# Two-layer graph network on one core: 16-bit count sums widened by ScalarE, the first power alone, a merge step inside a wait, the first aggregate's halves taken together

## The reference

```
# layer block 0: graph convolution, batch norm, gelu, twice the input added, layer norm
deg  = segment_sum(ones, col)            # reference adds one loop per node again
norm = rsqrt(deg)[row] * rsqrt(deg)[col]
h    = segment_sum(norm * (x @ W.T)[row], col) + b
h    = gelu(batch_norm(h, gamma, beta)) + x
x    = layernorm(x + h)
# layer block 1: two gated relational layers over 2 edge types
w[r] = sum_b att[r, b] * basis[b]        # 30 bases of 512 x 512 each, per layer
msg  = sigmoid(x_j @ gate_w[r]) * x_j @ w[r]      # r is the edge's type
h    = relu(segment_sum(msg, row) + x @ root1 + bias1)
out  = the same with basis2, att2, gate_w2, root2, bias2 on h
return layernorm(x + out)
```

## Time and profile before

| | |
|---|---|
| three runs | 316.65, 318.35, 320.71 us |
| median | 318.35 us |
| the profiled execution | 318.3 us |
| its span in the profile | 316.2 us |
| TensorE busy | 278.1 us, 88% of the span |
| VectorE, ScalarE, GpSimd busy | 161.4, 87.4, 40.3 us |
| mean granted clock of TensorE | 0.957 of full |
| moved by DMA | 73.63 MB |

### The profile page before, as it was taken

How to read it: one execution, slowest core, us unless ns; L and a number is a source line. 1 busy time by engine, 2 the same in 40 slices (tenths; PEclk the granted TensorE clock), 3 DMA queues, 4 the chain that set the end, 5 groups by cost and what they waited for, 6 DMA issues and landing times.

```text
span 316.2 us, 4593 instructions
## 1 busy us (share of the span) xinstructions
PE 278.1 (88%) x1687; PEld 184.8 (58%) x1687; DVE 161.4 (51%) x362; ACT 87.4 (28%) x137; POOL 40.3 (13%) x76
## 2 busy tenths in 40 slices
PE   1698958999699987659999999999997999999991
PEld 1583423343487554236766646677775777787770
DVE  3888888884575842983320141342425125334443
ACT  5250220201145848445152114111312242100000
POOL 2001000000294104510000000000004600010000
PEclk9999996999859997899999999999999999999997
DMA  6997992999938999986994977977101400001112
GB/s 174 241 417 295 338 403 82 410 379 401 367 86 274 343 421 419 423 313 262 335 399 158 421 287 288 425 282 262 77 0 43 126 0 0 0 2 32 32 32 65
DMA packets 12802, 73.63 MB, mean 233 GB/s; under 512 B 2000, under 2 KB 2243, under 8 KB 4588
## 3 DMA queue, kind: packets, MB, share of 16 engines
q1 hardware_dynamic: 11330, 70.82, 59.1%
q0 software_dynamic: 1104, 2.36, 2.7%
q10 hardware_dynamic: 346, 0.17, 0.2%
HBM read 72.05 MB, written 1.28 MB: 232 GB/s over the span
## 4 chain that ended last, share of the span: by engine, by line
PE 66%; DVE 12%; DMA 9%; issue 6%; DVEq 3%; SPq 1%; ACT 1%; POOL 1%; POOLq 0%; ACTq 0%
PE psW L495 15%; PE psM L476 9%; PE psM L478 8%; PE psM L477 8%; PE psM L720 7%; PE psM L740 6%; DMA basis_ring<-in_L_gnn_basis_dram 5%; DVE B L1037 3%; DMA w_raw<-in_L_gnn_W_dram 3%; PE psM L617 3%; PE psE L576 2%; PE psM L543 2%; DVEq L1027 2%; DVE oh_key L1044 1%; PE psM L599 1%
## 5 line engine op out<-in xcount | busy, mean ns | idle before, releaser
L495 PE MATMUL psW<-basis_ring,S 128*32 128x512 f32 x512 | 64.8, 624 | 5.4 <-DMA basis_ring<-in_L_gnn_basis_dram 3.3
L1216 DVE SCALAR_TENSOR_TENSOR zg<-psM,gate,zg 125x512 fp32r<-125x512 f32 x20 | 15.0, 750 | 56.9 <-ACT zg L893 56.9
L495 PEld LDWEIGHTS psW<-basis_ring,S 128*32 128x32 f32 x512 | 13.6, 112 | 38.8 <-issue 29.0
L476 PE MATMUL psM<-w,hlT 128*125 128x512 f32 x80 | 32.4, 406 | 0.1
L478 PE MATMUL psM<-w,hlT 128*125 128x512 f32 x80 | 31.7, 396 | 0.0
L477 PE MATMUL psM<-w,hlT 128*125 128x512 f32 x80 | 31.6, 395 | 0.0
L576 PEld LDWEIGHTS psE<-oh_key,oh_src 128*125 128x125 f16 x162 | 14.2, 146 | 22.4 <-issue 15.2
L893 ACT ACTIVATE zg<-psM,gate 125x512 fp32r<-125x512 f32 x20 | 13.8, 689 | 46.3 <-PE psM L478 45.9
L720 PEld LDWEIGHTS psM<-BB,zg 125*128 125x128 f32 x160 | 23.1, 188 | 3.4 <-issue 2.5
L720 PE MATMUL psM<-BB,zg 125*128 125x320 f32 (+1 forms) x160 | 24.1, 309 | 0.0
L740 PE MATMUL psM<-zg,BB 125*125 125x512 f32 x100 | 24.0, 394 | 0.0
(11 more groups left out here) (152 smaller groups left out, 383.2 us busy)
## 6 DMA issues: line engine op xcount, KB each, us to landing
basis_ring<-in_L_gnn_basis_dram SPq DMA_DIRECT2D x64, 1024.0 KB, 6.9
root_raw<-in_L_gnn_root_dram POOLq DMA_DIRECT2D x32, 64.0 KB, 2.1
xs<-in_x_dram SPq DMA_DIRECT2D x1, 1120.0 KB
out_dram<-xs SPq DMA_DIRECT2D x5, 224.0 KB
w_raw<-in_L_gnn_W_dram SPq DMA_DIRECT2D x4, 256.0 KB, 9.2
bias_b<-in_L_gnn_bias_dram POOLq DMA_DIRECT2D x1, 250.0 KB, 3.8
xs<-in_x_dram SPq DMA_DIRECT2D x1, 130.0 KB
out_dram<-xs SPq DMA_DIRECT2D x5, 26.0 KB
```

Source lines behind the costliest of these rows:

```text
L476: nc.tensor.matmul(o, l_hi, r_hi, start=start, stop=False)
L495: m = nc.tensor.matmul(psW[32 * j:32 * j + 32, cc % 2, :], S[:, cc % 2, cc // CH, q].rearrange("p k r -> p (k r)"), ring[:, n % RING, j, : ...
L1216: link(v.scalar_tensor_tensor(out=zg[:, 1, c, r, :], in0=bank(("Z", L, c, r))[0:PC, :], scalar=gate[:, L, c, r:r + 1], in1=zg[:, 0, c, r, ...
```

## The change

- **Counts.** The sums of chunks 1, 2 and 3 are written by VectorE as 16-bit numbers into memory of the one-hots (`at_sums`), and ScalarE widens them into `AT`. Chunks 0 and 4 are added directly as before. VectorE's order is 1, 2, 0, 3, 4; TensorE's degree matmuls go in the order 1, 0, 2, 3, 4, and each group waits for its own chunk (`wait_at`).
- **Powers.** GpSimd takes the power of the first column alone, then of the other four. ScalarE and VectorE start `z` of chunk 0 on the first. The five `diag` products become one of 625 elements.
- **Merge.** The second merge is cut in two. Its first step stands between the count sums and the wait for the degrees, the rest between the degree copy and `z`.
- **First aggregate.** For f = 0 both halves are taken together, chunk by chunk; the `dinv` matmuls come behind both. The bank uses of `dinv` move likewise.
- **Weight parts.** A pair of parts (20, 21) now stands ahead of the first aggregate. The pairs behind f = 0, 1, 2, 3 go up to 23, 25, 27 and 27 instead of 21, 23, 27 and 29.

```diff
         for f in range(KC):
             for h in range(2):
                 use(("agg0", f, h), "dve")
-                if (f, h) == (0, 0):
+                if (f, h) == (0, 1):
                     for i in range(2):
                         use(("dinv", i), "act")
...
+        SUMMED = (1, 2, 3)
+        AT_ORDER = (1, 0, 2, 3, 4)
+        def at_sums(c):
+            at = SUMMED.index(c) * BW
+            return oh_key[0:PC].rearrange("p t k -> p (t k)").bitcast(U16)[:, at:at + N2]
+        def wait_at(eng, c):
+            if c in SUMMED:
+                eng.wait_ge(at_from_sum, SUMMED.index(c) + 1)
+            else:
+                eng.wait_ge(at_ready, [a for a in range(NC) if a not in SUMMED].index(c) + 1)
+        FIRST_IN = 23
...
             pool.wait_ge(deg_ready, 1)
-            nc.gpsimd.tensor_tensor(dinv_p[:], deg[:], mhalf[0:PC, 0:NC], ALU.pow).then_inc(dinv_ready, 1)
-            pool.wait_ge(dinv_ready, 1)
+            for c in (slice(0, 1), slice(1, NC)):
+                nc.gpsimd.tensor_tensor(dinv_p[:, c], deg[:, c], mhalf[0:PC, c], ALU.pow).then_inc(dinv_ready, 1)
+            pool.wait_ge(dinv_ready, 2)
+            shape = [PC, NC, PC]
+            nc.gpsimd.tensor_tensor(diag[:], ident[0:PC, 0:PC].unsqueeze(1).broadcast_to(shape),
+                                    dinv_p[:].unsqueeze(2).broadcast_to(shape), ALU.mult).then_inc(diag_ready, 1)
...
-            for f in range(KC):
-                for h, (a, n) in enumerate(HALF):
+            basis_upto(21)
+            def aggregate0(f, halves):
+                for h in halves:
                     wait_free(pe, ("agg0", f, h))
-                    for s in range(NC):
-                        pe.wait_ge(z_ready, s + 1)
+                for s in range(NC):
+                    pe.wait_ge(z_ready, s + 1)
+                    for h in halves:
+                        a, n = HALF[h]
                         for i in range(2):
...
+            aggregate0(0, range(2))
+            pe.wait_ge(diag_ready, 1)
+            for i, (c0, c1) in enumerate(((0, 4), (4, NC))):
...
+            basis_upto(FIRST_IN)
+            for step in range(2):
+                counts_turned(step)
+            for f in range(1, KC):
+                for h in range(2):
+                    aggregate0(f, (h,))
+                    counts_turned(2 * f + h)
+                basis_upto((None, FIRST_IN + 2, 27, 27)[f])
             basis_upto(31)
...
+            for c in SUMMED:
+                act.wait_ge(at_sum, SUMMED.index(c) + 1)
+                nc.scalar.activation(AT[:, c], at_sums(c), ACT.Copy).then_inc(at_from_sum, 1)
...
-            act.wait_ge(dinv_ready, 1)
             for c in range(NC):
+                act.wait_ge(dinv_ready, 1 if c == 0 else 2)
                 nc.scalar.activation(z[:, 0, c, :], xw[:, c, :], ACT.Copy, scale=dinv_p[:, c:c + 1]).then_inc(z_hi, 1)
...
-            for c in range(NC):
-                v.tensor_tensor(AT[:, c], B[:, c, 0, 0:N2], B[:, c, 1, 0:N2], ALU.add).then_inc(at_ready, 1)
+            def counts_of(c):
+                sums = at_sums(c) if c in SUMMED else AT[:, c]
+                v.tensor_tensor(sums, B[:, c, 0, 0:N2], B[:, c, 1, 0:N2], ALU.add) \
+                    .then_inc(at_sum if c in SUMMED else at_ready, 1)
+            for c in (1, 2, 0, 3, 4):
+                counts_of(c)
+            w_merge_first(1)
             wait_full(dve, "deg")
             link(v.tensor_copy(deg[:], bank("deg")[0:PC, 0:2 * NC:2]))
             dve.sem_inc(free_dve, 1)
             dve.sem_inc(deg_ready, 1)
-            dve.wait_ge(dinv_ready, 1)
+            w_merge_rest(1)
             for c in range(NC):
+                dve.wait_ge(dinv_ready, 1 if c == 0 else 2)
...
-            w_merge(1)
             dve.wait_ge(dinv_b_ready, 2)
```

More of the change, by code:

```diff
@@ L215, in gnn_block @@
         at_ready, dinv_ready, dinv_b_ready = sem("at_ready"), sem("dinv_ready"), sem("dinv_b_ready")
+        at_sum, at_from_sum = sem("at_sum"), sem("at_from_sum")
         z_hi, z_ready = sem("z_hi"), sem("z_ready")
@@ L425, in _ @@
             pool.wait_ge(deg_ready, 1)
-            nc.gpsimd.tensor_tensor(dinv_p[:], deg[:], mhalf[0:PC, 0:NC], ALU.pow).then_inc(dinv_ready, 1)
-            pool.wait_ge(dinv_ready, 1)
+            for c in (slice(0, 1), slice(1, NC)):
[4 more added lines that the diff above has]
+                                    dinv_p[:].unsqueeze(2).broadcast_to(shape), ALU.mult).then_inc(diag_ready, 1)
             for c in range(NC):
-                nc.gpsimd.tensor_scalar(diag[:, c, :], ident[0:PC, 0:PC], dinv_p[:, c:c + 1], None, ALU.mult) \
-                    .then_inc(diag_ready, 1)
-            pool.wait_ge(at_ready, NC)
+                wait_at(pool, c)
             for kc in range(KC):
@@ L595, in _ @@
             wait_free(pe, "deg")
-            for s in range(NC):
-                pe.wait_ge(at_ready, s + 1)
+            for s in AT_ORDER:
+                wait_at(pe, s)
                 for c in range(NC):
                     last[0] = nc.tensor.matmul(bank("deg")[0:PC, 2 * c:2 * c + 2], AT[:, s, c * PC:(c + 1) * PC],
-                                               ones_r[:, 0:2], start=(s == 0 and c == 0),
-                                               stop=(s == NC - 1 and c == NC - 1), skip_group_check=True)
+                                               ones_r[:, 0:2], start=(s == AT_ORDER[0] and c == 0),
+                                               stop=(s == AT_ORDER[-1] and c == NC - 1), skip_group_check=True)
             done()
@@ L619, in _ @@
                                                        stop=(s == NC - 1 and i == 1))
-                    done()
[L621 to L637, removed]
@@ L638, in _, with counts_turned @@
-                basis_upto((21, 23, 27, 29)[f])
+                        if s == NC - 1:
+                            done()
+            def counts_turned(step):
+                for b in BB_STEPS[step]:
+                    wait_free(pe, ("bb", b))
+                    o = bank(("bb", b)).bitcast(BF16)
+                    for i, q in enumerate(range(4 * b, min(4 * b + 4, NC * R * NC))):
+                        d, t, s = q // (R * NC), q // NC % R, q % NC
+                        last[0] = nc.tensor.transpose(o[0:PC, i * P:i * P + PC],
+                                                      B[:, s, t, d * PC:(d + 1) * PC].bitcast(BF16),
+                                                      ident16[0:PC, 0:PC])
+                    done()
@@ new lines, in _ @@
+            aggregate0(0, range(2))
+            pe.wait_ge(diag_ready, 1)
+            for i, (c0, c1) in enumerate(((0, 4), (4, NC))):
+                wait_free(pe, ("dinv", i))
+                for c in range(c0, c1):
+                    last[0] = nc.tensor.matmul(bank(("dinv", i))[:, (c - c0) * PC:(c - c0 + 1) * PC],
+                                               ones_f[0:PC, :], diag[:, c, :], start=True, stop=True)
+                done()
+            basis_upto(FIRST_IN)
+            for step in range(2):
+                counts_turned(step)
@@ L1001, in w_merge, with w_merge_first @@
             def w_merge(pp):
+                w_merge_first(pp)
+                w_merge_rest(pp)
+            def w_merge_first(pp):
                 dve.wait_ge(w_half, R * (pp + 1))
@@ L1008, in w_merge, with w_merge_rest @@
                                        op0=ALU.mult, op1=ALU.add).then_inc(w_both, 1)
+            def w_merge_rest(pp):
                 link(v.scalar_tensor_tensor(out=half[:, 1, :], in0=psW[:, 1, :], scalar=mask_h[:, 0:1],
```

1 line of the change is left out of this document (removed).

## The result

The changed kernel takes 314.67 us (median of 11 runs, 312.48 to 315.80); the kernel before, measured beside it, 317.27 us (11 runs, 316.06 to 320.71). The ratio is 0.990, 95% interval 0.987 to 0.993: faster by 1.0%, within the 2% that count as no change here. The profiled execution took 314.59 us with a span of 312.7, against 318.3 and 316.2.

A forecast was written before the change was run, and what follows sets the result against it. TensorE's low-clock idle stretch and ring waits before 142 us were taken as the bound. Degrees +0.4 (hidden by power -0.6), third block -3.1, fourth and tail -1.7, transposes -0.5: 5.3 us off 318.3 gives 313.0, range 309.5 to 317.

The forecast's parts named there:

- The cause: Parts 20 and 21, used at 88.0 and 89.7 instead of 97.7 us, let later parts load in the empty stretch.
- The counts: Degree matmuls: 16-bit sums gain 1.0 us on VectorE, hidden behind TensorE; ScalarE's widening delays them, costing 0.4 us.
- The 16-bit add: Count sums: an add of 626 elements takes 0.48 us instead of 805 ns; the widening on ScalarE takes 0.80.
- The powers and `diag`: On GpSimd: first power result 0.6 us earlier, second power 1.05 us; single `diag` product 1.9 us, bounds 1.5 and 3.7.
- The merge as a gate: Ahead of the first aggregate: parts 20 and 21 wait for the merge, starting at 86.4 us, not 84.9.
- The clock at the aggregate: Pair takes 3.2 us at the low clock, full clock back about 91.1; aggregate ends at 93.6, `dinv` takes 1.1.
- The ring: Weight-part loads: part 31 lands near 113.4 us, not 121.55, and TensorE's three waits, 3.3 us in all, disappear.
- The end: From the transposes onward, a constant lead of 5 us to the end.
- the sooner clock: Rival at the first aggregate: pair runs at full clock, `dinv` ends 1.9 us earlier; time 311.1 us, chance 0.24.
- The ring rival: Root loads share the stretch with parts 24 and 25; part 31 only 2 us earlier, gain 1.5, 316.8 us, chance 0.09.
- GpSimd's low parts: Rival: three root-matrix low parts, 1.5 us each, delay the first layer-statistics power; 3.9 us remain, 314.4 us, chance 0.16.
- The slower case: Low clock lasts from 84.3 us into the second and third block; 318.9 us if back at 106; chance 0.04.

The follow-up runs named there:

- e1: Changed kernel with the weight parts back in their old places, none ahead of the first aggregate: 317.22 us, ratio 0.9997 to the kernel before.
- e2: Kernel before with only the pair of parts ahead of the first aggregate, later parts shifted and second merge split: 315.17 us, ratio 0.990 to the kernel before.
- e12: Kernel before with only the pair ahead, the split merge and idle matmuls (32-bit sums, one power, halves apart): within 0.3% of e10.
- e4: Changed kernel with the 16 root1 loads issued by SyncE ahead of part 24 instead of by GpSimd: 314.57 us, ratio 0.990 to the kernel before.
- e9: The changed kernel itself measured and profiled again, in the third group: 314.77 us.
- e3: Changed kernel with the whole second merge ahead of the degree copy: 315.35 us, ratio 0.992 to the kernel before.
- e8: Changed kernel with the first block's halves apart again, `dinv` matmuls behind the first: 312.90 us, ratio 0.985 to the kernel before.
- e5: Changed kernel with idle matmuls into a dead bank ahead of part 20, the first two x1 turns and part 36: 313.26 us, ratio 0.987 to the kernel before.
- e10: Changed kernel with both the idle matmuls of e5 and the halves apart of e8: 314.24 us, 0.998 of the changed kernel.

## Why the prediction was right, and where it was not

Direction and range held: forecast 313.0 (309.5 to 317), measured 314.67. The forecast was 5.3 us; the medians show 2.6, half of it. The time came out nearer than the gain by luck: the forecast started from 318.3, and over eleven runs the kernel before takes 317.27, from which 5.3 us less would have been 312.0. Step by step:

- **The cause.** "This stage's gain sits in the ring" and the pair in idle time: the pair is shown to be the cause by e1, which undoes it, and e2, which does it alone. That the gain runs through the ring is read from single profiles.
- **The counts, +0.4.** Missed. The degree copy starts 4.58 us after the first add, 4.50 before: +0.1. TensorE did start 0.43 later, but the 25 matmuls then took 3.15 us, where the kernel before took 3.50. In seven of the ten kernels with 16-bit sums they take 2.86; in the other three (3.15, 3.23, 3.70) the granted clock falls to the lower level under the last of them. My step "TensorE paces them as much as VectorE does" was read wrong out of the earlier trace rows: no wait is recorded in front of the later groups, and yet the adds set their pace. The kernels with all sums in 32 bits and a comparable start, e2 and e12, take 3.51 and 3.57 like the kernel before, and in its trace the weight loads of these matmuls pause at each chunk (busy 3.07 of 3.50 us), while in e4 they run without a pause (2.75 of 2.75 us). The estimate from the Trainium skill's "TensorE: Matmul & The Clock Gate", section "LDWEIGHTS (loading the stationary operand)", is 2.6 us. I had left it out of the sum, and it lies nearer to the measured 2.86 than my 3.5 does. Hidden from the end either way, as e2 shows.
- **The 16-bit add.** Right: 0.48 us long, two in 0.88. The widening took 0.72, not 0.80.
- **The powers and `diag`.** Two powers in 1.55 us (1.65 forecast). `diag` took 1.23 us, below my lower bound of 1.5; hidden.
- **The merge as a gate.** Right: TensorE waits 1.65 us for it, and part 20 starts 6.7 us after the first add, as forecast. That it is 6.7 to the tenth is luck: the degree copy was 0.3 us sooner and the merge behind it 0.3 us longer than I had them, and in e9 it is 7.3. But this gate has no price at the end: e3 takes 1.2 us of it away and gains nothing.
- **The clock at the aggregate.** Right: the pair took 3.64 us at the low level (3.2 forecast), the clock was back at 89.7 (forecast near 91.1), the 20 aggregate matmuls took 3.31 (3.9) and `dinv` 1.28 (1.1).
- **The ring, the step that failed first.** "Part 31 lands near 113.4": it landed at 117.67, and part 27 at 107.73, not by 101. My "some 24" us for eight parts and the root loads left 4 us of DMA time for the latter. That is what they took when little else was moving: in the kernel before, 131 GB/s at a share of 0.49 from 90.6 to 97.3 us, so 3.9 us for their 1.05 MB. Beside full ring loads DMA ran at 298 GB/s for 12 us. At the 419 GB/s of ring loads alone, the rest of those bytes is about 6 us, which leaves about 6 and not 4 for root1. What else makes part 31 late is not worked out; in part DMA was not full from 86.7 to 89.7 us (share 0.59). So "the three waits, 3.3 us, are gone" became 2.5 us left. The price is small, because ScalarE held the transposes almost as long. The last Gelu ended 38.6 us after the first add, as forecast (38.8), and parts 30 and 31 held the transposes 1.1 us more. So from that add the residual sums lead by 4.4 us, not 5.3; that the transposes started at 118.71 for 118.5 forecast hides it, since 0.66 us of that is the earlier first add.
- **The end, the step that failed second.** "Then a constant lead of 5 us to the end": the sum had no term for the clock after the residual sums. The low clock under parts 36 and 37 took 1.6 us of the lead, in both profiles of the changed kernel (3.51 and 3.54 us) and in e2 (3.58). It isn't there in e1, e4 and e8 (1.92), and why not is open. e5 and e10 show that this is not one wait to be filled: with dense work in it the stretch lies on the root products instead.

Of the rivals, the sooner clock did not come in the changed kernel; in e5 it did, and parts 22 and 23 came 1.6 us earlier (13.1 against 14.6 from the first add), but not in e10 and e12 with the same idle matmuls, and with no gain that held up beside the change. The ring rival (316.8) was half right: part 31 landed 3.9 us earlier, not 2, and most of the waits stayed. GpSimd's low parts delayed nothing: the first power started 0.3 us behind its variance, and the next did not wait. The slower case did not occur.

## What to carry to other kernels

When a stage alternates between empty and full DMA time, look for work that frees a buffer during the empty part; here this one move carried the whole change, and shortening the chain beside it gave nothing that could be measured. Price a load by the DMA time that it takes in the trace (share times length), not by its bytes, and allow for more when it shares the engines with a full stream: root1 took 3.9 us nearly alone and about 6 beside the ring. Do not take a gain from two single profiles: e1 and the kernel before have nearly the same median, and their profiled executions differ by 2.8 us, as much as the whole change. And compare candidates only within a group that also holds the version they are to beat: e5 and e8 looked 0.3% and 0.5% better than the change in a group without it, and their mixture was equal to it in the next.

## What the runs showed of the hardware that was not expected

- The 16 root loads, 1 MB in all, slow a full DMA stream to 298 GB/s (GpSimd's queue, 89 to 101 us) or 230 GB/s (SyncE's, 89 to 94 us) at a share of 0.95 to 1.00, where ring loads alone run at 406 to 423. Nearly by themselves, in the kernel before, they moved 131 GB/s at a share of 0.49 (90.6 to 97.3 us), 267 for a full share.
- Back-to-back matmuls with no recorded wait can still be paced by their producer: 25 take 3.50, 3.51 and 3.57 us behind 32-bit adds, and 2.86 behind the mixed ones as long as the clock stays full (seven kernels of ten).
- GpSimd's product of 625 elements with both operands broadcast took 1.23 us, less than its 1.54 for 512 elements in a permuted layout.
- Idle matmuls in front of a wait did not remove a low-clock stretch further on. It moved: 137.4 to 141.1 us in the changed kernel, 131.2 to 138.5 in e10. And in e12 the clock stayed at the lower level (0.51) from 83.0 to 89.9 us, although TensorE was busy all of it.
- The same wait doesn't always meet the same clock: behind 2.1 us of idle time the pair 36/37 took 1.92 us in the kernel before and in e8, 3.51, 3.54 and 3.58 in both profiles of the change and in e2.
